# Weight sums that start behind the second token tile, in a fused attention and FFN kernel

## The reference

```python
def reference(x, Wq, bq, Wk, bk, Wv, bv, Wo, bo, router_w, w1, b1, w2, b2):   # x: 4 x 1024 x 1024
    xn = layernorm(x)
    # attention branch: 16 heads of 64, linear, all elementwise
    phi_q, phi_k = elu(xn @ Wq.T + bq) + 1, elu(xn @ Wk.T + bk) + 1
    kv_sum = cumsum(phi_k * (xn @ Wv.T + bv), axis=1)          # over the 1024 tokens of a sequence
    s = (phi_q * kv_sum * 64 ** -0.5) @ Wo.T + bo
    # FFN branch: top 2 of 8 experts, 256 places each; all experts share w1 and w2
    probs = softmax(xn @ router_w.T); top_p, top_i = top_k(probs, 2)
    # a pick beyond the 256th of its expert is dropped
    h = gelu(rows_kept @ w1.T + b1) @ w2.T + b2
    g = silu(sum over kept picks of h * top_p)
    return x + s * g
```

## Time and profile before

| | |
|---|---|
| Median of 3 runs | 2017.0 us (2015.99 to 2017.03) |
| The profiled execution | 2017.51 us |
| Its span, first to last instruction | 2015.4 us |
| Granted TensorE clock, mean | 0.995 |
| Busy: TensorE, VectorE, ScalarE, GpSimd | 1974.4, 1373.3, 698.2, 510.2 us |

### The profile page before, as it was taken

How to read it: one execution, slowest core, us unless ns; L and a number is a source line. 1 busy time by engine, 2 the same in 40 slices (tenths; PEclk the granted TensorE clock), 3 DMA queues, 4 the chain that set the end, 5 groups by cost and what they waited for, 6 DMA issues and landing times.

```text
span 2015.4 us, 27129 instructions
## 1 busy us (share of the span) xinstructions
PE 1974.4 (98%) x9396; PEld 905.4 (45%) x9396; DVE 1373.3 (68%) x2089; ACT 698.2 (35%) x1094; POOL 510.2 (25%) x640
## 2 busy tenths in 40 slices
PE   9989999999999999999999999999999999999995
PEld 2345555555444444444444444444444444444442
DVE  3788887888777767777777797564555455456656
ACT  1432222223654344344345343433212212222322
POOL 0088888887003212311110010120000000000002
PEclk9999999999999999999999999999999999999998
DMA  9576666667798988877777879673332333334535
GB/s 357 205 251 229 212 224 215 229 232 219 240 362 262 261 275 264 260 249 266 239 239 253 279 236 319 222 210 114 105 104 95 106 103 97 118 105 161 179 121 119
DMA packets 185258, 419.92 MB, mean 208 GB/s; under 512 B 18816, under 2 KB 73664, under 8 KB 182720
## 3 DMA queue, kind: packets, MB, share of 16 engines
q1 hardware_dynamic: 141776, 287.93, 43.1%
q0 software_dynamic: 34912, 121.71, 20.0%
q10 hardware_dynamic: 8464, 8.92, 1.4%
HBM read 268.51 MB, written 166.77 MB: 216 GB/s over the span
## 4 chain that ended last, share of the span: by engine, by line
PE 89%; DVE 5%; issue 2%; DMA 1%; ACT 1%; SPq 0%; POOL 0%; DVEq 0%; ACTq 0%; POOLq 0%
PE pair L2069 34%; PE pair L2040 32%; PE pair L1879 16%; PE pair L1829 2%; PE pair L1908 1%; PE pair L1930 1%; PE pair L2009 1%; DMA spare<-up_sums 0%; PE pair L1842 0%; DMA routing<-kvs_dram 0%; DMA arena<-x_t 0%; DVE xnT L1492 0%; DMA spare<-w_up 0%; DVE arena L1605 0%; DVE arena L1265 0%
## 5 line engine op out<-in xcount | busy, mean ns | idle before, releaser
L2069 PE MATMUL pair<-arena 128*128 128x512 f16 x3360 | 729.9, 379 | 3.4 <-DVE arena L1630 1.2
L2040 PE MATMUL pair<-xnT,arena 128*128 128x512 f16 x2400 | 525.4, 379 | 5.4 <-ACT arena L1059 2.5
L2069 PEld LDWEIGHTS pair<-arena 128*128 128x128 f16 x3360 | 327.9, 98 | 402.1 <-issue 7.6
L1630 DVE SCALAR_TENSOR_TENSOR arena<-pair,arena 128x1024 f32<-128x1024 f32 x234 | 286.0, 1223 | 155.7 <-PE pair L2069 155.1
L1879 PE MATMUL pair<-arena 128*128 128x512 f16 x1728 | 384.4, 380 | 2.9 <-DVE xnT L473 2.1
L1072 ACT ACTIVATE arena<-arena 128x512 f16<-128x512 f32 x280 | 171.3, 626 | 559.7 <-PE pair L2069 505.0
L2040 PEld LDWEIGHTS pair<-xnT,arena 128*128 128x128 f16 x2400 | 234.6, 98 | 289.7 <-ACT arena L1059 3.4
L1879 PEld LDWEIGHTS pair<-arena 128*128 128x128 f16 x1728 | 168.9, 98 | 196.5 <-issue 4.8
L2040 PE MATMUL pair<-xnT 128*128 128x512 f16 x960 | 213.7, 379 | 0.0
L1605 DVE SCALAR_TENSOR_TENSOR arena<-arena 128x512 f16<-128x512 f32 x280 | 189.0, 687 | 17.6 <-ACT arena L1072 16.9
L800 POOL DMA_DIRECT2D s_dram<-arena x8 | 6.2, 777 | 596.5 <-DVE arena L1630 596.5
(11 more groups left out here) (213 smaller groups left out, 1816.6 us busy)
## 6 DMA issues: line engine op xcount, KB each, us to landing
down_dram<-arena SPq DMA_DIRECT2D x70, 512.0 KB, 5.9
arena<-down_dram SPq DMA_DIRECT2D x70, 512.0 KB, 3.3
up_dram<-arena SPq DMA_DIRECT2D x100, 256.0 KB, 5.6
arena<-up_dram SPq DMA_DIRECT2D x100, 256.0 KB, 2.6
arena<-down_sums SPq DMA_DIRECT2D x40, 512.0 KB, 6.6
arena<-w_up POOLq DMA_DIRECT2D x38, 512.0 KB, 5.4
up_sums<-arena POOLq DMA_DIRECT2D x38, 512.0 KB, 3.9
arena<-w_down POOLq DMA_DIRECT2D x32, 512.0 KB, 5.5
```

The costliest lines, as they stand in the source:

```text
L1630: ins = nc.vector.scalar_tensor_tensor(to, src, scale, to, ALU.mult, ALU.add)
L2040: ins = mm(out_to, w[:, a, c * P:(c + 1) * P], x_in_op[:, b, c, :], start=(first and i == 0), stop=(i == 11), skip_group_check=True)
L2069: ins = mm(down_banks(j, t // 2)[:, (t % 2) * BLOCK:(t % 2 + 1) * BLOCK], g_ops[:, A_NAMES.index(DOWN_A[j]), c, a, t * P:(t + 1) * P], dow ...
```

## The change

Three things. GpSimd waits for `kvlo_ready` 6, the end of the second token tile, before the first unit, and 18 units instead of 10 run in the down groups, three in each of the first six. In the second tile ScalarE reads all four parts of the selection, and VectorE's two reads are gone; VectorE's statistics there stand in the same place as before. And in SyncE's queue both halves of the last block of x stand ahead of the weight blocks 12 to 15.

```diff
--- before.py
+++ after.py
@@ -181,7 +181,7 @@
         DOWN_AT = {"11": 0, "22": 2, "21": 3, "T2": 0, "T3": 1, "T1": 2, "T4": 3}
 
 
-        LATE_UNITS = 10
+        LATE_UNITS = 18
         late_sums = xnT_rows[:, 8:12, HOLE:2 * HOLE]
 
 
@@ -501,7 +501,8 @@
             for b, weights in ((2, (1, 2)), (3, (3, 4)), (4, (5, 6)), (5, (7, 8)), (6, (9, 10, 11)), (7, (12, 13, 14, 15))):
                 for half in range(2):
                     load_xt(b, half)
-                    for q in weights[half::2]:
+
+                    for q in weights[half::2] if b < TOKEN_BLOCKS - 1 else weights * half:
                         load_wkv(q)
 
             sp.wait_ge(wkv_ready, SOON + 1)
@@ -784,6 +785,8 @@
             in_time = len(UNITS) - LATE_UNITS
             load_unit(0)
             load_unit(1)
+
+            pool.wait_ge(kvlo_ready, 6)
             for u in range(in_time):
                 make_unit(u)
                 if u + 2 < in_time:
@@ -821,15 +824,15 @@
                             meta[:, t, :], None, bounds_check=SLOTS - 1, oob_is_err=False).then_inc(meta_stored, 16)
                     pool.dma_start(out_rows[i, p], x_rows[i, p]).then_inc(copied, 16)
 
-                    u = in_time + 2 * i + p // 4
-                    if u < len(UNITS):
-                        if p % 4 == 0:
+                    u = in_time + 3 * i + p // 2
+                    if u < len(UNITS) and p < 6:
+                        if p % 2 == 0:
                             if u == in_time:
                                 pool.wait_ge(xsum_done, 32)
                             else:
                                 pool.wait_ge(sum_stored[(u - 1) % 3], 16 * ((u - 1) // 3 + 1))
                             load_unit(u)
-                        elif p % 4 == 2:
+                        else:
                             make_unit(u)
 
             pool.wait_ge(meta_stored, 16 * TILES)
@@ -924,7 +927,7 @@
                 copy(act_scratch[:, :], zero_c[:, :]).then_inc(x_filled, 1)
                 act.wait_ge(x_filled, 1)
 
-            def tile(t, u, first=False):
+            def tile(t, u, first=False, second=False):
                 def exp_k(half):
                     act.wait_ge(proj_read, 4 + 4 * t + half + 1)
 
@@ -936,10 +939,11 @@
                 if not first:
                     exp_k(0)
                 at = act.value_load(start_i[0:1, ds(t + 2, 1)], min_val=0, max_val=SLOTS)
-                for s in (0, 2):
+                for s in range(4) if second else (0, 2):
                     act.wait_ge(stage_done, 5 * t + 4 + 1 + s + 1)
                     apart(act)
-                    read_selected(copy, 1 - u, s, 2 + (u + 1 + s) % 2, ds(at, P), stage_act)
+
+                    read_selected(copy, 1 - u, s, 2 + (u + 1 + s) % 2, ds(at, P), stage_dve if s % 2 else stage_act)
                     if s == 0 and not first:
                         exp_k(1)
                 if first:
@@ -964,7 +968,7 @@
                     high_x()
 
             tile(0, 0, first=True)
-            tile(1, 1)
+            tile(1, 1, second=True)
             with act.Fori(1, pairs) as g:
                 for u in range(2):
                     tile(2 * g + u, u)
@@ -1447,10 +1451,10 @@
                     if not second:
                         stats_x(u, t + 3, 16 * g + 32)
                     read_k(1)
-                    read_odd(1)
                     if second:
                         stats_x(u, t + 3, 16 * g + 32)
-                        read_odd(3)
+                    else:
+                        read_odd(1)
                     prepare()
                     places()
                     phi_k()
```

## The result

The changed kernel takes **2013.81 us** (2012.31 to 2015.93, 18 runs), beside 2017.38 (2014.55 to 2022.01, 18 runs) for the kernel before on the same chip: a ratio of 0.998, with a 95% interval of 0.9974 to 0.9986. It is faster by about 0.2%; I had forecast 2008.6, in a range of 2006.5 to 2012.8, and the time lies above that range. The profiled execution took 2013.8 us, its span is 2011.6, 3.8 shorter than before. Lines up to about 500 stand as before, those behind them 1 to 4 lines further down (L1879 is L1883, L2040 is L2044, L1003 is L1007, L1511 is L1515).

What follows compares the result with a forecast made beforehand. TensorE, busy 98% of the span, was taken as the bound, so only its gaps count: 1.1 + 1.2 + 0.8 + 2.3 - 0.2 + 2.5 + 0.8 = 8.5, taken as 8.4, giving 2008.6 us; range 2006.5 to 2012.8 (own 2006.9 to 2010.2).

Steps and rivals of the forecast that it cites:

- Eight more units in the down groups: Late GpSimd units in the down groups: a chain of three fits a 73 us group; cost 0, at worst 1 us.
- Slower: Rival, chance 0.05: late units stretch VectorE's steps on the path; all 32 sums would end at 2025.6 us.
- worst-case sum: Down groups: 8 units x 4 sums, each stretching one VectorE step on the path by 0.53 us: 17 us.
- The last block of x: Last block of the scores: second half issued at 57.7 instead of 64.15, closing TensorE's gap, 1.1 us gained.
- The second and third tile: TensorE's gaps there close: 1.2 + 0.8 + 2.3 - 0.2 in the second tile, 2.5 + 0.8 around the third.
- The low part of x of the third tile: VectorE's step, at 139.51 before, was to start at about 130.8, leaving out the shift of 1.1.
- The clock: Third tile: with the 2.3 us gap gone, no fall of the granted clock behind it; 1.7 us gained, 1.00 expected.
- The clock falls anyway: Rival, chance 0.08: gaps of 0.6 to 0.8 us remain at 97 and 103, 1.7 us stay; 2010.3 us.
- VectorE stays late: Rival, chance 0.08: GpSimd is not what stretches VectorE, so only the four instructions go; 2013.5 us.
- ScalarE becomes the bound: Rival, chance 0.11: selection 3, then the third tile's start, wait 1 to 2.5 us for parts 1 and 3; 2010.7.
- the 0.2 us at selection 3: Second tile: selection 3 needs ScalarE's read of part 1 and starts about 0.2 us late, a cost.
- The sums in front: GpSimd's 62 units ahead of the late ones, from some 137 us, end at 494 us, at no cost to TensorE.

Runs made afterwards that it cites:

- second pair of profiles: Repeat profiles of the unchanged kernel before and the unchanged changed kernel on one chip; single time 2020.31 us for before, median 2016.63 us for changed.
- late_only: Kernel before with only the late part, 18 late units, three in each of six down groups: 2025.55 us, ratio 1.0025.
- third_no_sums: Changed kernel with the third unit's additions in the first four down groups over 8 columns instead of 256, transfers whole: 2009.84 us, ratio 0.9951.
- third_behind: Changed kernel, all sums made, third unit's additions in the first four groups waiting until the quad's head is past: 2010.43 us, ratio 0.9955.
- head_ten_late: Changed kernel with 10 late units, two in each of five groups as before, the rest as changed: 2017.57 us, ratio 0.999.
- after_again: The changed kernel, unchanged, run and profiled once more: 2016.63 us, ratio 0.9986.
- behind_again: The kernel of third_behind, unchanged, run once more on the same chip as after_again: 2010.91 us, ratio 0.9956.
- before_again: The kernel before, unchanged, profiled a second time on the same chip as after_again: one time, 2020.31 us.
- three relatives: third_behind with GpSimd's wait, ScalarE's reads or the load order undone, one each: 2017.53, 2011.93 and 2013.58 us.

## Why the prediction failed, point by point

**The step that failed** is "Eight more units in the down groups", with its "Cost 0": it costs 4.0 us (5.4 in the second pair of profiles, 7.7 in late_only). What I had named as its bound from above, and as the rival *Slower* with a chance of 0.05, is what happens, at 4 of its 17 us: VectorE's steps with two inputs in SBUF are stretched by 0.53 us each beside GpSimd's additions, three or four of them in a row on the path, in four groups. third_no_sums removed only additions, third_behind only moved them, and late_only had nothing else of the change; all three agree. So it is shown that these additions, at this place, cost the time. That they do it by way of VectorE is read from the trace: the stretched steps stand ahead of each gap, and its size follows their number.

The evidence that misled me was true: ten units opened no gap, and VectorE had 20 of 73 us free. But a third unit lies at another place than the first two. Before, the additions of the first of a group began in the middle of the down products (612.68), those of the second 3 us into the first quad (633.75); the third begins at the head of the second quad (640.12, its first product stands at 642.00), where VectorE, ScalarE and TensorE pass one product on with about 0.3 us to spare (a delay of 1.04 made TensorE's row 0.73 late). I had written this down as what speaks for the rival and weighed it with the mean idle time of VectorE. In the last two of the six groups GpSimd's third unit began sooner in the group (927.20 and 997.04 us, 45.5 and 42.8 us behind the start of the down group, where the first of the six has 52.5), and there is no gap. My worst-case sum, 8 units x 4 sums x 0.53, was too high for the same reason: it is not the number of sums but their place.

The Trainium skill, GPSIMD Engine Reference, Key points, has the rule that GpSimd shares its SBUF interfaces with VectorE and contends where VectorE has two SBUF inputs. The traces agree in the late units too, and for the other kind of step: VectorE's L1629, with one input in PSUM, took 1.23 us from 603.35 on in the changed kernel, beside two additions of 0.72 and 0.73 us, and takes 1.22 beside none:

```profile
600.76 1.22 DVE L1629 SCALAR_TENSOR_TENSOR arena<-pair,arena 128x1024 f32<-128x1024 f32 x1
...
603.35 1.23 DVE L1629 SCALAR_TENSOR_TENSOR arena<-pair,arena 128x1024 f32<-128x1024 f32 x1 [0.77 <-PE pair L2073]
```

This may also be a reason why the first unit of a group is cheap, which no run tries: about every other step of VectorE beside the down products is of that kind, while the five steps at the head of the quad that are shown above all have two inputs in SBUF.

**What held.** The last block of x: 1.1 forecast; the gap is gone, and undoing the order alone brings 1.07 back. The second half was issued at about 58.0, forecast 57.7. The second and third tile: 7.4 net forecast, 7.55 measured (26.17 less 18.62); by parts, GpSimd's wait is worth 5.9 on top of the rest and ScalarE's reads 2.05. Together that is more than 7.55, since either also covers a part of what the other wins. The low part of x of the third tile starts at 130.17, forecast 130.8 less 1.1, so 0.5 later. The clock: 1.00, as forecast, so the rival *The clock falls anyway* is out for the tile, and so is *VectorE stays late*. *ScalarE becomes the bound* is out as well: the 0.2 us at selection 3 did not appear, and ScalarE releases nothing from 114 to 133 us. Selection 2 began at 123.47, so selection 3 was due at 123.91, and ScalarE had ended part 1 at 123.79, 0.1 us ahead of it. The sums in front: the last store is issued at 487.28, forecast 494. The store of the last late unit is issued at 1000.67 and landed by 1005.6, forecast 1020: the chain of three units took 43.6 us from the first load's issue (961.94), forecast 56.

**What was mis-sized beside it** is the range. The entry takes 59.3 and 60.3 us in two profiles of before, 60.7 and 59.3 in two of the changed kernel, and from 58.9 to 62.3 over all profiles of this study but head_ten_late's, which took 63.0 (my expectation for after_again had overlooked it). In all but that one a gap of 1.0 to 3.8 us stands near 550, released by ScalarE at the line that is L1063 in the changed kernel:

```profile
550.45 12.22 PE L2044 MATMUL pair<-xnT,arena 128*128 128x512 f16 x48 [2.51 <-ACT arena L1063]
```

In some executions the clock falls behind it (granted 0.89 from 545 to 560 us in the changed kernel's profile, 0.77 in behind_again's, 1.00 in before's):

```profile
545.00:560.00 15.00, 12.49 (x51) 5.15 (x50) 12.72 (x19) 11.47 (x20) 0.00 (x0) 0.89 1.00 365
```

The DMA engines are wholly busy there (share 1.00, 365 GB/s). So the 1.35 us at the entry in the first pair are not put down to the change: the second pair shows 1.0 with the other sign. The three profiles with the head as it was (before, before_again, late_only) take 59.5 in the mean, the nine others without head_ten_late 60.6, and the two groups overlap. What decides this gap from one execution to the next, and whether the earlier quads make it longer, stays open; I tried nothing on it. My own range of 3.3 us took in none of this. The time lies 5.2 us above the forecast. The late units are 4.0 of that and would have given 2012.6, just inside the stated range; the entry adds 1.35 and the stretch behind the groups takes off 0.9, and the kernel before has a median 0.4 higher over 18 runs than over the three that the forecast started from.

**The sum as the first pair of traces gives it:** 2017.5 - 8.3 + 4.0 + 1.35 - 0.9 = 2013.65, the profiled 2013.8. The best kernel of the study that makes all sums is third_behind, at ratios 0.9955 and 0.9956: it keeps the head and pays less for the late units, nothing in one profile and 1.5 to 3.7 us in those of its repetition and its three relatives.

## What to carry to other kernels

When work of GpSimd is moved, don't ask how much idle time VectorE has in the mean but beside which instructions each addition will run, and how much slack the chain there has to TensorE; a kernel in which the same work is already hidden proves it only for its own place. Start GpSimd's side work behind the stretch in which VectorE is on the path, and if it can't end in time then, put the rest by a wait beside a stretch in which VectorE has slack, not at the first free slot of the queue. Then look at the loads of that stretch in more than one profile: here the first profile showed the new place as free, and four others did not. And undo a change part by part: here three parts that win hid one that costs half as much.

## What the runs showed of the hardware

- In the rows above, a VectorE step with two SBUF inputs of 128x512 goes from 0.69 to 1.22 us and one of 128x1024 from 1.22 to 1.75, both by 0.53, beside GpSimd additions of 128x256. I had not expected the larger step to lose no more. The amount is not fixed everywhere: a step of 128x512 took 0.88 us at 623.42 and another 0.75 at 625.38 in the same trace, and VectorE's L1476 took up to 1.62 in the token tiles where its shortest is 0.68.
- It goes both ways, and a single step of VectorE can pass unstretched while the addition pays. GpSimd's additions took 0.93, 1.11, 1.59 and 1.17 us beside those steps, the 1.59 beside the step of 128x1024, and 0.72, 0.73 and 0.73 where they were moved to (a fourth took 1.71). At 604.66 a VectorE step with two SBUF inputs took its normal 0.69 us, and the addition beside it 1.15.
- Steps of VectorE that read one of their inputs from PSUM were never stretched: in all thirteen profiles none of 128x512 that ran beside an addition took more than 0.69 us, none of 128x1024 more than 1.23.
- The same load of sums took from 3.4 to 7.8 us from issue to use, in a stretch (660 to 735 us) whose DMA share was 0.87 to 0.94 in all thirteen profiles.
